# A state-space mixer's pair loop: outputs read before the C sum, a swap before later row loads, one step per head for skip and sum

## The reference, cut to what matters

```python
Bh = rope(rms(Braw) + B_bias, phi)      # phi = cumsum(dt) * rope_freqs, per head
Ch = rope(rms(Craw) + C_bias, phi)
u = xh * dt
h = a_t * h + u_t (x) b_t               # state, per head: 8 x 64
y = einsum('bhpn,bhn->bhp', h, c_t)     # for every token
y = SSD_SCALE * ys + D_param * xh       # the skip term
g = y * silu(z)                         # then a norm and W_out
```

## Time and profile before

| | us |
|---|---|
| median of 3 runs | 1564.37 |
| lowest and highest run | 1563.4 and 1566.02 |
| the profiled execution, its own time | 1572.69 |
| its span in the trace | 1570.9 |
| PE busy / DVE busy / ACT busy / POOL busy | 1332.1 / 1128.3 / 907.6 / 435.1 |
| pair loop of batch 0, first products to the scan's last reader | about 415 to 730 |
| pair loop of batch 1 | about 1186 to 1502 |

### The profile page before, as it was taken

One profiled execution on the slowest core, in us unless ns is written; L12 is line 12 of the kernel. 1 busy time (PEld: TensorE's weight loads), 2 busy tenths in 40 slices (PEclk: granted clock), 3 DMA queues, 4 the chain that ended last, 5 costly groups with the idle time before them and its releaser, 6 DMA issues.

```text
span 1570.9 us, 39585 instructions
## 1 busy us (share of the span) xinstructions
PE 1332.1 (85%) x15736; PEld 797.0 (51%) x15816; DVE 1128.3 (72%) x1823; ACT 907.6 (58%) x1527; POOL 435.1 (28%) x415
## 2 busy tenths in 40 slices
PE   5688888899789999998846889888987999999985
PEld 3533322345466666666625333323454666666663
DVE  4678981545599999996566677633376999999937
ACT  3524447544578777884326245563355888888741
POOL 4799930132122222222124000002312222222201
PEclk9678999899899999999967799998997999999998
DMA  5000001300722222221010000000016222222100
GB/s 167 1 2 3 1 2 36 107 1 14 135 50 61 53 53 53 53 59 38 1 54 2 29 2 2 2 1 27 1 52 111 57 54 53 57 60 57 42 1 27
DMA packets 37614, 62.04 MB, mean 39 GB/s; under 512 B 15088, under 2 KB 25072, under 8 KB 36992
## 3 DMA queue, kind: packets, MB, share of 16 engines
q1 hardware_dynamic: 37216, 58.44, 15.8%
q10 hardware_dynamic: 288, 2.10, 0.3%
HBM read 19.75 MB, written 7.01 MB: 17 GB/s over the span
## 4 chain that ended last, share of the span: by engine, by line
PE 52%; DVE 16%; issue 13%; ACT 12%; POOL 2%; DVEq 2%; DMA 1%; POOLq 1%; ACTq 0%; SPq 0%
DVE region L1195 5%; PE PS L1585 4%; PE PS L1695 4%; PE PS L1647 4%; PE PS L1707 4%; PE PS L1834 3%; PE PS L1819 3%; PE PS L1850 3%; ACT L1024 3%; PE PS L1597 3%; PE PS L1867 2%; PE PS L1943 2%; PE PS L1627 2%; DVE S L1390 2%; PE PS L1873 2%
## 5 line engine op out<-in xcount | busy, mean ns | idle before, releaser
L791 POOL TENSOR_TENSOR region<-region 128x1024 f32<-128x1024 f32 x64 | 155.2, 2426 | 517.1 <-DVE region L1378 517.1
L886 ACT ACTIVATE region<-PS 128x512 f32<-128x512 f32 x288 | 164.7, 597 | 130.7 <-PE PS L1647 88.8
L1195 DVE TENSOR_REDUCE region<-PS 128x1 f32<-128x512 f32 (+3 forms) x304 | 180.7, 652 | 69.1 <-PE PS L1600 44.2
L1834 PEld LDWEIGHTS PS<-region 64*64 64x64 f32 x4096 | 136.8, 135 | 40.0 <-issue 40.0
L1834 PE MATMUL PS<-region 64*64 64x64 f32 x4096 | 154.4, 224 | 0.0
L1597 PE MATMUL PS<-region 96*128 96x512 bf16 (+3 forms) x384 | 117.7, 358 | 25.2 <-DVE region L1195 17.3
L1647 PE MATMUL PS<-region 99*128 99x512 bf16 x288 | 112.6, 412 | 19.8 <-ACT region L886 19.0
L1383 DVE TENSOR_TENSOR region<-region 128x1024 f32<-128x1024 f32 x64 | 117.6, 1838 | 0.0
L1375 DVE SCALAR_TENSOR_TENSOR region<-region,rows 128x1024 f32<-128x1024 f32 x64 | 82.2, 1284 | 45.1 <-DMA region<-region 26.7
L1002 ACT ACT_TABLE_LOAD x60 | 77.0, 1283 | 61.9 <-PE PS L1794 35.6
L728 POOL TENSOR_TENSOR coef<-var,power 128x4 f32<-128x4 f32 (+2 forms) x16 | 16.2, 1011 | 340.1 <-DVEq L1112 340.1
(11 more groups left out here) (258 smaller groups left out, 2935.6 us busy)
## 6 DMA issues: line engine op xcount, KB each, us to landing
region<-region SPq DMA_DIRECT2D x256, 128.0 KB, 2.4
region<-parts_scratch SPq DMA_DIRECT2D x8, 448.0 KB, 9.8
X<-in_L_attn_x_dram SPq DMA_DIRECT2D x2, 1024.0 KB, 5.7
region<-in_L_ffn_factors_dram SPq DMA_DIRECT2D x2, 1024.0 KB, 7.0
out_dram<-X SPq DMA_DIRECT2D x4, 512.0 KB, 2.9
parts_scratch<-region SPq DMA_DIRECT2D x2, 768.0 KB, 4.3
w_in_s<-in_L_attn_W_in_dram SPq DMA_DIRECT2D x1, 1216.0 KB, 7.9
region<-in_L_ffn_W_fc_dram SPq DMA_DIRECT2D x1, 1024.0 KB, 6.1
```

The source lines that it names most:

```text
L791: nc.gpsimd.tensor_tensor(PB1[:, r], PB1[:, r], PB2, ALU.add).then_inc(s_bb, 1)
L886: nc.scalar.activation(PB[:, u % (2 * G0), :], PS[:, 2 + u % 2, :], ACT.Exp).then_inc(s_p, 1)
L1195: nc.vector.reduce_max(MB[:, h:h + nh, k0 // 4], src, AX).then_inc(s_smu, 1)
L1834: last = mm(PS[q, 2 + half, (i % 4) * P + 64 * c:(i % 4) * P + 64 * c + 64], PB1[q, r, t], PC1[q, r, t], start=True, stop=True, tile_posit ...
```

## The change

- SP: `swap(1, 1)` now comes ahead of the rows of the later groups. These come in pieces: group 1 right behind that swap on a semaphore of its own (`s_mv1`), then two groups after each of the first three swaps of the unrolled turn. PE waits for `s_mv1` ahead of the first phases of group 1, and for all of `s_mv` ahead of the hardware loop.
- ACT and PE ahead of the loop: the phases and sines of pair 1 come between the projections of tiles 6 and 7, not behind both.
- DVE: in `products` the wait for `s_yt` stands ahead of the third multiplication, not the first.
- DVE: `pair_outputs` is cut in two. `add_carried` (carried part times decay, plus the direct part) stands ahead of `rotated_c`; `add_direct` stands behind it and does skip term and sum in one step per head, four steps of 64 elements per lane in place of two of 256.
- PE: `turn(n, 1)` moves ahead of `gram(n, 0)`, and `turn_outputs(n - 1)` moves from the end of the slot to the place ahead of `chunk_sums(n)`.

```diff
@@ SP, ahead of the loop and in its unrolled turn
-                load_rows(1, PAIRS // 4, s_mv)
                 swap(1, 1)
+                load_rows(1, 2, s_mv1)
-                def slots(it, last):
+                def slots(it, last, first=False):
                     for k in range(4):
                         if not (last and k >= 2):
                             swap(it * 4 + k + 2, k)
+                        if first and k < 3:
+                            load_rows(2 * k + 2, 2 * k + 4, s_mv)
@@ ACT, ahead of the loop
-                for i in (6, 7):
-                    copy_x(i)
+                copy_x(6)
                 sines(1, 1)
+                copy_x(7)
@@ DVE, products
-                    dve.wait_ge(s_yt, at(b, n, 2))
                     (PB1 and PB2)
+                    dve.wait_ge(s_yt, at(b, n, 2))
                     (PC1 and PC2)
@@ DVE, pair_outputs
-                def pair_outputs(n):
+                def add_carried(n):
                     nc.vector.tensor_tensor(YT, y[:, 0], e, ALU.mult)
-                    nc.vector.tensor_tensor(own, own, d, ALU.mult)
                     dve.drain()
                     nc.vector.tensor_tensor(YT, YT, y[:, 1], ALU.add)
+                def add_direct(n):
                     dve.drain()
-                    nc.vector.tensor_tensor(own, own, YT, ALU.add).then_inc(s_yd, 2)
+                    for e in range(4):
+                        last = nc.vector.scalar_tensor_tensor(own[:, :, e, :], own[:, :, e, :], dpar[:, bass.ds(n * 2 + e, 1)],
+                                                              YT[:, :, e, :], ALU.mult, ALU.add)
+                    last.then_inc(s_yd, 2)
@@ DVE, slots
+                        if k % 2 == 1 and not (first and k == 1):
+                            add_carried(n - 3)
                         rotated_c(n, k)
                         if k % 2 == 1 and not (first and k == 1):
-                            pair_outputs(n - 3)
+                            add_direct(n - 3)
@@ PE, slots
                         decay_args(it, k, not (last_ and k >= 2))
+                        turn(n, k, 1)
                         gram(n, k, 0)
-                        turn(n, k, 1)
                         gram(n, k, 1)
+                        if not (first and k == 0):
+                            turn_outputs(n - 1, k + 3)
                         chunk_sums(n, k)
                         if first and k == 1:
-                            pe.wait_ge(s_mv, (b + 1) * 4 * 16)
+                            pe.wait_ge(s_mv1, (b + 1) * 4 * 16)
                         (phases)
-                        if not (first and k == 0):
-                            turn_outputs(n - 1, k + 3)
@@ PE, ahead of the loop
-                (project_x(6), project_x(7), then phases(0, 1) and phases(0, 2))
+                (project_x(6), phases(0, 1), project_x(7), phases(0, 2))
                 slots(0, True, False)
+                pe.wait_ge(s_mv, (b + 1) * 12 * 16)
```

More of the change, by code:

```diff
@@ L438, in build @@
         s_mv0 = sem("first_rows_loaded")
+        s_mv1 = sem("second_rows_loaded")
         s_mv = sem("rows_loaded")
@@ L604, in slots @@
                             swap(it * 4 + k + 2, k)
-                slots(0, False)
+                        if first and k < 3:
+                            load_rows(2 * k + 2, 2 * k + 4, s_mv)
+                slots(0, False, True)
                 with sp.Fori(1, LAST) as it:
@@ L1403, in pair_outputs @@
                     y = PS[:, 7, :].rearrange("p (y t e d) -> p y t e d", y=2, t=NT, d=HD)
-                    own = XS[:, :, bass.ds(n * 16, 32)].rearrange("p t (e d) -> p t e d", d=HD)
-                    d = dpar[:, bass.ds(n * 2, 4)].unsqueeze(1).unsqueeze(3).to_broadcast([P, NT, 4, HD])
                     nc.vector.tensor_tensor(YT, y[:, 0], e, ALU.mult)
-                    nc.vector.tensor_tensor(own, own, d, ALU.mult)
                     dve.drain()
                     nc.vector.tensor_tensor(YT, YT, y[:, 1], ALU.add)
+                def add_direct(n):
+                    own = XS[:, :, bass.ds(n * 16, 32)].rearrange("p t (e d) -> p t e d", d=HD)
                     dve.drain()
-                    nc.vector.tensor_tensor(own, own, YT, ALU.add).then_inc(s_yd, 2)
+                    for e in range(4):
+                        last = nc.vector.scalar_tensor_tensor(own[:, :, e, :], own[:, :, e, :], dpar[:, bass.ds(n * 2 + e, 1)],
+                                                              YT[:, :, e, :], ALU.mult, ALU.add)
+                    last.then_inc(s_yd, 2)
                 def slots(it, first, last):
@@ L1431, in _ @@
                 mixing(PAIRS - 1, 3)
-                pair_outputs(PAIRS - 2)
+                add_carried(PAIRS - 2)
+                add_direct(PAIRS - 2)
                 def gate(i):
@@ L1920, in _ @@
                 expand(NT - 1)
[L1921 to L1927, removed]
+                pe.wait_ge(s_tkc, b + 1)
+                project_x(6)
+                pe.wait_ge(s_t1, b * PAIRS + 1)
+                phases(0, 1)
+                project_x(7)
+                pe.wait_ge(s_t1, b * PAIRS + 2)
+                phases(0, 2)
                 pe.wait_ge(s_xv, (b + 1) * NT)
```

## The result

The median of the changed kernel is 1539.04 us (1534.41 to 1541.39), of the kernel before beside it 1565.19 (1563.4 to 1566.37). The ratio is 0.983, with an interval of 0.9805 to 0.9856. The forecast of 1554.0 was 15 us too slow, and its range ended 3 us above the result: the sign was right, the size was not. The profiled execution took 1539.18 us.

What follows compares the result with a forecast made beforehand. DVE paced the loop at 38.15 us per turn, PE and ACT close behind; a DMA wait stood ahead of it. Saving 11.4 ahead less 1.0 in the loop, 10.4, gave 1564.37 - 10.4 = 1554.0 us; range 1542 to 1562.

Steps and rivals of the forecast that it cites:

- Ahead of the loop: Before the hardware loop: pair 1's swap no longer queues behind row loads, saving 5.7 us per batch, 11.4 in all.
- DVE's turn: Hardware loop on DVE: odd slots save 0.47 us each, so four slots go from 38.15 to 37.2 us.
- the four at 0.80: DVE at odd k: four new steps of 64 elements in `add_direct`, priced at 0.2 us each, 0.8 together.
- PE's slot of 9.0 us: Hardware loop on PE: at k of 2 and 3, 9.28 us less the 0.26 wait ahead of `chunk_sums` leaves 9.0.
- The turn of 38.2: Hardware loop: four slots on PE take 2 * 9.98 + 9.2 + 9.0 = 38.2 us, so PE and not DVE paces.
- the ring of PE and ACT with its late sines: Hardware loop: PE waits for sines whose table load follows the phases at k of 0 and 1, slots 9.32 to 9.98 us.
- a loss of 1 us: Hardware loop: 12 turns staying at 38.2 us, plus the odds at the loop's end, cost 1 us in sum.
- the unrolled turn, whose moves I let cancel: Rest of the unrolled turn ahead of the hardware loop: the moves were said to about cancel, so no gain was counted.
- DVE as the pace: Hardware loop: sines not late for PE, turn 37.2 us, 11.4 us more won, 1542.5; chance 0.17.
- The slower case, the late load in all four slots: Hardware loop at `decay_args`: sines' table load behind the phases in every slot, turn 39.9 us, time 1574; chance 0.10.

Runs made afterwards that it cites:

- the part ahead of the loop alone: Kernel before plus SP's new order and the new places of pair 1's phases and sines, loop unchanged: 1554.87 us, ratio 0.9899.
- SP's order alone: Kernel before plus only the swap of pair 1 first, row loads in pieces and PE's waits for the rows: 1557.15 us, ratio 0.9931.
- the split of the B sum: Changed kernel with late C-sum wait and early sines table load, plus B sum shared at even k (POOL 704 columns, DVE 320): 1524.92 us, ratio 0.9726.
- the kernel with both: Changed kernel with the C-sum wait moved to the third product and ACT's waits swapped for an early sines table load: 1526.44 us, ratio 0.9727.

## Why the prediction was wrong

**Ahead of the loop: right.** I took 11.4 us (5.7 per batch, where my own 4.2 and 1.7 add up to 5.9), and that part alone gave 10.5 up to O4. The second products at 421.91 came 2.6 us ahead of the 424.5 of the forecast, because the first ones and POOL's sum began earlier too (417.31, where before has 420.00); POOL released them, and the clock stayed full, as forecast. That the sines of pair 1 need not come earlier for this, as the prediction has it, SP's order alone shows.

**DVE's turn: right, a little too long.** I had 37.2 and it is 37.05. The odd slots save 10.62 - 10.09 = 0.53 and 10.05 - 9.67 = 0.38, 0.455 in the mean where I had 0.47. That this is so near is in part luck. The C sum is free of POOL, but it saves only 0.36 and 0.34 from its start to the next step's and not 0.51, as `add_direct` starts 0.23 after its end. The other steps save 0.17 and 0.04 together, where I had a loss of 0.04 with the four at 0.80; they take 0.87. The even slots, at 8.66 and 8.63 where I read 8.74, save 0.1 each. I had said that the wait moved within `products` gains nothing there; the idle time ahead of the first product is 0.24, and 0.34 in before. That the moved wait does this was not tried alone.

**The step that failed: PE's slot of 9.0 us, "and 9.0 is left".** The turn of 38.2 was 2 * 9.98 + 9.2 + 9.0, and each of the four terms rests on PE's work in a slot, which I summed at 9.02 (5.74 less the wait of 0.26, plus 0.67, plus 2.87) and which is 8.61. The kernel with one half of `turn` back between the two of `gram` parts the difference of 0.41, as its slot without a wait is 8.79. The 0.18 from there to 8.61 is the order of `turn` and `gram`: I said of `turn` in the loop nothing at all, and so priced it at nothing. The other 0.23 both kernels have: the wait ahead of `chunk_sums`, 0.26 in its row, was 0.34 by the starts (576.90 less 575.44 and the 1.12 that the half of `gram` takes), and `turn_outputs` cost 0.52 in the new place (577.67 to 578.19), not 0.67. In after, the 0.31 that `decay_args` to `turn_outputs` is shorter does not come through in full: `chunk_sums` starts 0.65 behind `turn_outputs`, at 574.23, and ACT's second `turn_copy`, for which it waits, ends at 574.18; where that copy ends earlier, at 555.36, it is 0.51 (555.21 to 555.72). Four times 0.41 is 1.64, and 38.2 - 1.64 = 36.6; with the wait for the C sum moved, a turn took 36.65. That the two agree is in part luck. PE's waits there are 2.1 us a turn, as in my sum, but 0.33, 0.87 and 0.43 for the sines at k of 0, 1 and 2 and 0.47 for DVE, where I had 0.96 at k of 0 and 1 and 0.2 at k of 2. So the ring of PE and ACT with its late sines is there, but PE's work in it was taken too long by 0.41 a slot, and so the sum put the ring behind DVE's 37.2, where it is a little ahead of DVE's 37.05. Even with `turn` between, where PE does set the pace, the turn is 37.5 and not 38.2.

**What that cost.** In place of a loss of 1 us the hardware loop won 6 * (1.07 + 0.81) = 11.3 and the last turns 1.0 (in both kernels one slot there has a granted clock of 0.57, so whose the 1.0 is stays open): 13.3 of the 16.6 us between the forecast of 10.4 and the 27.0 in the pair loops. The other 3.3 lie in the unrolled turn, whose moves I let cancel: from P0 to O4 both batches win 14.7 us together. There DVE does not set the pace yet, and PE's shorter slot is seen directly: O1 to O4 takes 26.5, 8.83 a slot, where the part ahead of the loop alone leaves 27.83, 9.28 a slot. It is the same term once more.

**The rivals.** DVE as the pace, at 1542.5, was the right one, with a chance of 0.17; it was 3.5 us above the result, of which the unrolled turn, which stood in it at nothing, accounts for 3.3. The evidence I named against it, that PE's waits are short because `turn_outputs` fills the time, was true but did not bear on it. The slower case, the late load in all four slots, did not come: late loads stayed at k of 0 and 1 (ACT's table load waits 0.17 us for the phases at 567.37 and 2.80 at 577.27).

**What stays open.** Why a `gram` in one piece takes 0.18 us less than in two is not shown, only that it does. Whether the split of the B sum beats the kernel with both by more than the times vary is not settled either.

## What to carry to other kernels

Where two engines are within a few per cent of each other, the forecast hangs on the sum of the one that is not the bound; build that sum from starts, and ask of every moved instruction what stands still ahead of it now and what will then stand ahead of it (the page's idle time per group names it, though not its price). Test each later bound with the smallest edit that takes its wait away: two moved waits were worth nothing and 6.1 us of the pair loops alone and 11.4 together, because each uncovered the other's bound. An order on one engine is worth nothing without the order on the engine that feeds it: `add_carried` early without `turn_outputs` early lost it all.

## What the hardware showed that I had not expected

- The weight loads of `gram` (64x64, f32) stood still for 0.43 us behind the bf16 matmuls of 512 columns of `decay_args` in before, and 0.17 ahead of the second piece: 40.0 us in all, and 11.1 in after, where f32 matmuls of `turn` stand between. PE's slot became 0.18 shorter by that order.
- A table load of 1.28 us stands behind the first of the two waits ahead of its activation. With the wait for the products first, PE's waits for the sines (0.30 to 0.87 us in after) were gone from the window; that was worth nothing as long as DVE was the pace.
- A first product of 1024 elements behind the C sum starts 0.24 us after its end when it waits for that sum, and 0.08 before its end when it does not: 0.32 us for a wait on a step that the same engine had just done.
